# Reordering the units of a decoder layer: when transposed probabilities are copied, where TensorE's side work stands, and when the per-token head maxima are taken

## The reference

```python
x = x + attn(layernorm(x), Wq, Wk, Wv, Wo)        # 16 heads of 32, causal over 512 tokens
x = x + xattn(layernorm(x), ctx, ctx)             # per token: 16 x 16 scores between heads, causal over heads
x = x + ffn(layernorm(x), W_int4, bias, A, B)     # 256 x 256, weights rounded to int4, rank 16 addition

# attn:  scores = q k^T / sqrt(16), causal, softmax, times v, times Wo
# xattn: q[s, q, :] . ctx[s, k, :] / sqrt(16), for each token s on its own, softmax over k, times ctx
```

## Time and profile before

| | us |
|---|---|
| median of 3 runs | 926.34 (923.63 to 928.44) |
| profiled execution, its time | 928.57 |
| its span in the trace | 926.5 |
| granted PE clock, mean over the span | 0.932 |
| busy: PE / weight loads / DVE / ACT / POOL | 711.5 / 576.6 / 631.8 / 611.4 / 480.2 |

### The profile page before, as it was taken

The page is one execution under the profiler, slowest core; times in us unless marked ns, Lnnn a source line. Parts: engine busy times, 40 slices in busy tenths (PEclk is TensorE's granted clock), DMA queues, the critical chain, the costliest instruction groups (busy, mean ns, idle before and its releaser), DMA issues.

```text
span 926.5 us, 15953 instructions
## 1 busy us (share of the span) xinstructions
PE 711.5 (77%) x5147; PEld 576.6 (62%) x5147; DVE 631.8 (68%) x1897; ACT 611.4 (66%) x1688; POOL 480.2 (52%) x449
## 2 busy tenths in 40 slices
PE   3777888777677767787677767787677797779997
PEld 2655667566555555666556555666556575559995
DVE  2544555577477758886568758886568787878873
ACT  4567776987388847877478847877478867762110
POOL 1000001263677664675577664675577847836542
PEclk9789899999799988999989989999989998979997
DMA  5856566576346725576536725576536653500001
GB/s 154 117 70 78 68 101 98 73 100 99 46 65 88 108 42 74 77 118 92 73 48 103 107 42 74 80 116 92 73 49 103 85 88 50 96 7 13 29 12 35
DMA packets 46980, 70.53 MB, mean 76 GB/s; under 512 B 4385, under 2 KB 21554, under 8 KB 46898
## 3 DMA queue, kind: packets, MB, share of 16 engines
q1 hardware_dynamic: 46898, 69.52, 50.3%
HBM read 14.98 MB, written 4.19 MB: 21 GB/s over the span
## 4 chain that ended last, share of the span: by engine, by line
PE 47%; ACT 18%; DVE 14%; issue 10%; POOL 6%; DMA 4%; SPq 1%; ACTq 0%; DVEq 0%; POOLq 0%
PE misc L453 21%; PE score_bank L453 10%; PE acc_bank L453 9%; ACT probs L819 8%; PE turn_bank L539 6%; POOL prod L1459 4%; DVE score_bank L1099 4%; DVE head_scores L1126 4%; DMA stack_k<-k_lo 4%; ACT probs_t L775 3%; PE turn_bank L453 2%; ACT inv_wide L775 1%; DVE attn_t L1121 1%; ACT x_in L782 1%; DVE ln_raw L1079 1%
## 5 line engine op out<-in xcount | busy, mean ns | idle before, releaser
L1099 DVE CUSTOM_DVE_ANT_0 score_bank<-score_bank,causal 128x384 f32<-128x384 f32 (+3 forms) x512 | 242.9, 509 | 113.7 <-PE score_bank L453 113.3
L819 ACT ACTIVATE probs<-score_bank,neg_max 128x384 f32<-128x384 f32 (+3 forms) x512 | 269.1, 538 | 76.8 <-DVE neg_max L1099 76.4
L775 ACT ACTIVATE probs_t<-turn_bank 128x512 f32<-128x512 f32 x320 | 193.9, 606 | 138.8 <-PE turn_bank L539 138.0
L539 PE MATMUL turn_bank<-ident,probs 128*128 128x128 f32 x1280 | 203.7, 283 | 16.0 <-ACT probs_t L775 14.9
L1459 POOL TENSOR_TENSOR prod<-head_probs,ctx_sb 128x256 f32<-128x256 f32 (+1 forms) x100 | 181.5, 1846 | 2.0
L539 PEld LDWEIGHTS turn_bank<-ident,probs 128*128 128x128 f32 x1280 | 150.9, 146 | 43.0 <-issue 29.9
L453 PE MATMUL score_bank<-stack_k,stack_q 96*128 96x384 f32 (+3 forms) x512 | 157.7, 369 | 25.9 <-DMA stack_k<-k_lo 12.7
L263 POOL TENSOR_TENSOR prod<-x1n,ctx_sb 128x256 f32<-128x256 f32 (+1 forms) x104 | 157.5, 1547 | 6.1 <-ACT x1n L782 6.1
L1408 POOL TENSOR_TENSOR ln_var<-ln_mv,eps 128x4 f32<-128x4 f32 x21 | 4.8, 228 | 259.9 <-DVE ln_mv L1087 259.9
L453 PE MATMUL acc_bank<-probs_t,values 128*32 128x384 f32 (+2 forms) x1280 | 79.2, 395 | 40.9 <-ACT probs_t L775 40.9
L819 ACT ACTIVATION_READ_ACCUMULATOR probs<-score_bank,neg_max 128x1 f32 x512 | 110.3, 215 | 0.0
(11 more groups left out here) (171 smaller groups left out, 1262.1 us busy)
## 6 DMA issues: line engine op xcount, KB each, us to landing
stack_q<-q_hi SPq DMA_DIRECT2D x64, 256.0 KB, 5.0
stack_k<-k_hi SPq DMA_DIRECT2D x64, 256.0 KB, 9.7
stack_q<-q_lo SPq DMA_DIRECT2D x32, 256.0 KB, 7.1
stack_k<-k_lo SPq DMA_DIRECT2D x32, 256.0 KB, 11.0
x_in<-in_x SPq DMA_DIRECT2D x9, 512.0 KB, 11.8
ctx_sb<-in_ctx SPq DMA_DIRECT2D x32, 128.0 KB, 2.1
x<-in_x SPq DMA_DIRECT2D x7, 512.0 KB, 7.5
out<-y_sb SPq DMA_DIRECT2D x5, 512.0 KB, 3.2
```

The lines of the kernel that those rows point to most:

```text
L539: last = nc.tensor.transpose(turn_bank[unit % 2][:, j * P:(j + 1) * P], probs[:, unit % RING, j * P:(j + 1) * P], ident[:, :])
L775: return nc.scalar.activation(dst, src, ACT.Identity)
L819: last = nc.scalar.activation(probs[:, unit % RING, at:at + width], score_bank[unit % 3][:, at:at + width], ACT.Exp, bias=neg_max[:, ring, ...
L1099: last = vec.tensor_tensor_reduce(v, v, causal[:, T - width:T], 1.0, 3.0e38, ALU.add, ALU.min, neg_max[:, ring, h, blk:blk + 1])
```

## The change

`LAG` stays 3 for PE's transposes, and a new `KEEP_LAG` of 4 says when ACT copies them: ACT now makes the exponential of unit n first and then copies the transposed unit n - 4. PE's side work is spread so that about one piece stands in a unit: it takes the transposes of a unit ahead of `attend`, moves `attend` to unit 4, `spread_inverses` to unit 6, `project_v` to units 5 and 7, and both halves of the output projection to group 0 units 8 and 9 (before: group 0 unit 9 and group 1 unit 2). The two `misc` banks are dealt out anew. The head maxima are taken in unit 1 of the following group, and POOL subtracts them there after the largest of its four products. The load of `x1` is issued by ACT rather than SP. Some layer norm pieces move by one or two units.

```diff
-    LAG = 3
+    LAG, KEEP_LAG = 3, 4
@@ PE, body
+                        if st["N"] and n < LAG or st["C"] and n >= LAG:
+                            turn_unit()
+                        if st["N"] and n == KEEP_LAG:
+                            attend(st["N"][1])
                         if st["A"] and n in (0, 1):
                             ...
                             project_qk(st["A"][1], n)
-                        if st["N"] and n == LAG:
-                            attend(st["N"][1])
-                        if st["N"] and n < LAG or st["C"] and n >= LAG:
-                            turn_unit()
-                        if st["N"] and n == LAG + 1:
+                        ...
+                        if st["N"] and n == 6:
                             spread_inverses()
-                        if g == 1 and ok(i - 1) and n == 2:
-                            output_projection(1)
...
-                        if g == 0 and ok(i - 1) and n == 9:
-                            pe.wait_ge(attn_ready, n_attn.up(NG))
-                            output_projection(0)
+                        if g == 0 and ok(i - 1) and n in (8, 9):
+                            if n == 8:
+                                pe.wait_ge(attn_ready, n_attn.up(NG))
+                            output_projection(n - 8)
@@ ACT, body
-                        if st["N"] and n < LAG or st["C"] and n >= LAG:
-                            keep_turned((n - LAG) % UNITS)
...
                         if st["C"]:
                             exponential(n, st["C"][1])
+                        if st["N"] and n < KEEP_LAG or st["C"] and n >= KEEP_LAG:
+                            keep_turned((n - KEEP_LAG) % UNITS)
...
+                            nc.scalar.dma_start(x1[:, :, :], x_t[i - 1]).then_inc(x1_loaded, 16)
@@ DVE, body
+                        if attended and n == 1:
+                            head_maxima()
...
-                        if g == 0 and i >= 0 and ok(i + 1) and n in (5, 7):
+                        if g == 0 and i >= 0 and ok(i + 1) and n in (4, 6):
...
+                        if g == 0 and ok(i - 1) and n == 9:
+
+                            dve.wait_ge(x1_loaded, n_x1.up(16))
+                            add_to_x1(0)
...
-                        if scored_tile and n == 9:
-
-                            dve.wait_ge(h_masked, n_masked.now())
-                            vec.tensor_reduce(head_max[:, :], head_probs[:, :, :], axis=AX_X,
-                                              op=ALU.max).then_inc(h_max, 1)
@@ POOL, body
-                        score_products(gp, t, range(CHUNKS)).then_inc(hqk_prod, 1)
+                        score_products(gp, t, (3,))
+                    if attended:
+                        shift_scores()
+                    if scored_tile:
+                        score_products(gp, t, (0, 1, 2)).then_inc(hqk_prod, 1)
```

More of the change, by code:

```diff
@@ L492, in ffn_low_rank, with transpose_tokens @@
                 last.then_inc(setup_pe, 1)
-            def transpose_tokens(src, sem_out, c, reader, count):
-                bank = take(c, reader, count)
+            def transpose_tokens(src, sem_out, c, which, reader, count):
+                bank = take(which, reader, count)
                 for t in range(NT):
@@ L500, in project_qk @@
             def project_qk(g, which):
-                bank = take(which, qk_lo_ready, r_lo)
+                bank = take(1 - which, qk_lo_ready, r_lo)
                 n = 0
@@ L510, in project_v @@
             def project_v(pair, half):
-                bank = take(1 - half, v_ready, r_v)
+                bank = take(1, v_ready, r_v)
                 for t in range(2):
@@ L558, in spread_inverses @@
                 pe.wait_ge(inv_spread, n_group.total)
-                bank = take(1, attn_ready, r_attn)
+                bank = take(0, attn_ready, r_attn)
                 for t in range(NT):
@@ L573, in ffn @@
             def ffn(half):
-                bank = take(half, y_ready, r_y)
+                bank = take(1 - half, y_ready, r_y)
                 for t in range(2):
@@ L617, in body @@
-                        if pair is not None and n in (6, 8):
-                            if i < 0 and n == 6:
-                                pe.wait_ge(w_lo_ready, 2)
-                            project_v(pair, n // 2 - 3)
-                        if (i, g) == (0, 1) and n == 7:
+                        if g == 2 and ok(i + 1) and n in (2, 4):
+                            if n == 2:
+                                pe.wait_ge(ln_done[0], n_ln[0].up(LN_PARTS))
+                            transpose_tokens(x_in, xt_psum, n // 2 - 1, 1, xt_ready, r_xt)
@@ L622, in body @@
+                        if pair is not None and n in (5, 7):
+                            if i < 0 and n == 5:
+                                pe.wait_ge(w_lo_ready, 2)
+                            project_v(pair, n // 2 - 2)
+                        if st["N"] and n == 6:
+                            spread_inverses()
+                        if (i, g) == (0, 1) and n == 8:
                             ffn_largest()
-                        if (i, g) == (0, 1) and n == 8:
+                        if (i, g) == (0, 1) and n == 9:
@@ L800, in keep_values @@
                 copy(values[:, 2 * pair:2 * pair + 2, 2 * half:2 * half + 2, :],
[L801 removed]
+                     misc[1][:, :].rearrange("p (t s n) -> p s t n", t=2, s=2)).then_inc(v_ready, 1)
             def other_weights():
@@ new lines, in body @@
+                        if g == 2 and ok(i + 1) and n in (3, 5):
+                            act.wait_ge(xt_psum, n_xt.up())
+                            copy(xt_hi[:, n // 2 - 1, :], misc[1][:, :]).then_inc(xt_hi_ready, 1)
+                        if st["N"] and n == 5:
+                            keep_acc()
+                        if pair is not None and n in (6, 8):
+                            keep_values(pair, n // 2 - 3)
+                        if g == 1 and ok(i - 3) and n in (8, 9):
+                            act.wait_ge(x2t_psum, n_x2t.up())
+                            copy(x2t_hi[:, n - 8, :], misc[9 - n][:, :]).then_inc(x2t_hi_ready, 1)
@@ L968, in _ @@
                 body(i)
-            for n in range(UNITS - LAG, UNITS):
+            for n in range(UNITS - KEEP_LAG, UNITS):
                 keep_turned(n)
@@ L1160, in body @@
                             take_max(n, st["C"][1])
+                        if g == 1 and ok(i - 1) and n == 0:
+                            add_to_x1(1)
                         if st["A"] and n in (1, 2):
```

152 lines of the change are left out of this document (70 added, 82 removed).

## The result

| | before | after |
|---|---|---|
| median, us | 926.31 (923.63 to 928.44, 4 runs) | 1040.2 (1037.75 to 1041.82, 4 runs) |
| span of the profiled execution | 926.5 | 1035.7 |
| granted PE clock, mean | 0.932 | 0.877 |

The changed kernel takes 1.123 times as long, 95% interval 1.119 to 1.127. The forecast was 917 us and the range 901 to 938, so it was wrong in its sign and far outside its range.

The account below looks back on a forecast made before the run. Chains from engine to engine bound the kernel, with DVE's 8 us wait for POOL. Terms of -21.1 on 928.57 gave 907.5; 12 for path changes and clock gave 919.5; less 2.2 to the median, 917 us, range 901 to 938.

Parts of the forecast that it names:

- the stall: DVE's wait in group 0 until POOL has masked the head scores: 8 us, gone five times, batches 2 to 6.
- the late copy: ACT's copy behind the exponential, one unit later: gives back some 3 us of a batch's gain in g2 and g3.
- a loop over two units: Maxima, exponential, copy, transpose, filler, scores, maxima: 3.37 us for two units of two pieces, plus PE's filler.
- four distances: Attend to attend: about 28 to 30 us in g0, 23 to 25 in g1, 23 to 24.5 in g2 and g3.
- The issue of x1's load: ACT asks for x1 in g0 n3; taken as costing nothing, hidden in slack below some 0.7 us.
- floor: Sums along one path at full clock: 98.4 us a steady batch, 907.5 in all; chance 0.25 that it is met.
- the other path: The path changes between odd and even units where fillers make the other heavier: some 0.5 us in a batch.
- second rival: The loop costs more than the stall gave, with attend at half clock in g0 and g1: 941 us, chance 0.23.
- one stretch in a batch: One further stretch of PE at the lower clock level in each of eight batches, 1 us each.
- a case with the clock at its full level: Without the stall PE would keep 2.4 GHz, so 1 us in each of eight batches is not spent: 909 us.
- Batch 0: The first batch, its groups short of attends and full of weight work: put at -1 us.
- fourth rival: ACT's wait for transposes, 138.0 us, was the real bound; ending it speeds every group: about 885 us, chance 0.07.

Follow-up runs that it names:

- the warm run: Changed kernel with five extra 128 wide matmuls of constants into `acc_bank` ahead of the transposes of unit 3 and of unit 4: 1012.75 us, ratio 1.092.
- the fastest kernel: Changed kernel with `KEEP_LAG` 3 and ACT's copy ahead of the exponential, attend in unit 3 behind the transpose: 856.88 us, ratio 0.920.

## Why the prediction was wrong

**What bounds the kernel, and the stall.** The reading of the stall was right: it goes, the row of `head_max` is gone, and taken alone the edit wins 32 us. That the late copy makes a loop over two units was right too: its links came out within 0.1 us of their forecast sizes, and PE waits for `probs_t` some 1 us in most units, as the prediction said it would. And g2 and g3 got longer, as it said. None of the four distances that it named held, though: 32.5 for 28 to 30 in g0, 26.8 for 23 to 25 in g1, 27.2 and 28.2 for 23 to 24.5. The issue of x1's load, for which it took nothing, takes ACT's queue 0.37 to 0.42 us, seven times.

**The step that failed** is the one behind the sums: "These are sums along one path with nothing else in its way, so they are a floor. Two things come on top", and then "1.5 us in each of eight batches". The measured time is not near that path: in batch 5 the distance to the floor is 114.7 - 98.4 = 16.3 us, not 1.5, and in batches 2 to 6 together 574.2 - 489.7 = 84.5, or 16.9 a batch. The late copy was put at some 3 us in g2 and g3 of a batch; the kernel before with it alone takes 100 us more (1027.6 against 927.8). The chain of one group, g3 to g0, can be read from the timeline above: attend to the maxima of unit 6, 6.81 (572.77 to 579.58); to those of unit 8, 4.91; DVE from there to unit 9, 1.66 (586.15); to those of unit 1, 6.39 (to 592.54); to its exponential 0.80; ACT itself to the exponential of unit 3, 5.26 (forecast 5.28); and to attend, 2.43. That is 28.26 where the forecast had 23.3. Of the 5.0 us between them:

- low clock 3.2: attend 3.54 for 2.30, the projection 2.71 for 1.39, a transpose 1.02 for 0.41. The mean granted clock of this stretch is 0.86, where the earlier trace rows has 1.00.
- the other path 1.8, the rest, of which 1.4 between attend and unit 9. The chain runs over the even units from attend on, not the odd ones, and it has a link that no sum had: the copy of unit 0 waits for attend (89.3 us in 31; here 576.52), then the transpose at 577.26 for the copy, then a projection of the values stands ahead of the scores at 579.15. Before, this copy stood ahead in ACT's unit 3 and waited for an attend of the same unit. Now it stands behind an exponential, in the unit after, with attend behind one more transpose, and PE's next transpose waits for the copy in turn.

For the other groups this wasn't taken apart; they are 3.5, 3.9 and 3.9 us over their floors, so the miss is of one size in all four, but its parts need not be. This is a comparison of lengths along one chain and not a test: the warm run takes attend's share of the clock away, and still stands 12.9 us over the floor in its batch.

**The clock was taken as a small correction to the loop, and it is part of it.** PE's waits of 1 to 1.8 us come just ahead of the transposes and of attend, and then attend, a filler of every group, runs long. I allowed one stretch in a batch. The second rival named this very mechanism, with attend at half clock in two groups, and gave 941; its own test, a clock under 0.85 in g0 and g1, did not come true (0.92 and 0.90). The clock was lowest in g3. By the warm run attend's part is 27 us of the 114. So the second rival had the direction and a part of the mechanism, not the size.

The Trainium skill (TensorE: Matmul & The Clock Gate, "What's actually happening") led me to a case with the clock at its full level, because the stall's end would keep PE busy. The rule on idleness agrees with the trace after, whose mean granted clock is 0.877 against 0.932; I had applied it to the one stall that went and not to the 213 waits that came. The Trainium skill's remark on repeating bubbles (Perfetto Trace Analysis, "Optimization Strategy"), that they can mean too few buffers, fits the 213 waits of 1.05 us. With two banks handed back a unit earlier the same edits take 857 to 878 us, so here the time of the release was enough. Whether a third bank would do as much isn't shown; it wasn't tried.

**Batch 0** was put at -1 without a sum and came out at +20.1. With the copy ahead its batch 1 starts at 130.2 us in the trace and not 147.9, so it is the same loss. I had treated it as short of attends and full of weight work, but the loop doesn't need attend.

**The price of the side work** was not seen either: the spread fillers, which the forecast counted only as weights in the loop, are worth 67 us where the loop isn't bound (926.6 to 859.7, with the statistics a unit earlier in it). ACT's wait for transposes falls from 138.0 us to 58.8 in the fastest kernel. That would fit my fourth rival (0.07, 885 us), which the late copy hides here, but it isn't shown that this wait carries the gain: DVE's wait for `q_hi` falls too, from 68.2 us to 14.7. Which of the moved fillers carries it is open as well.

**What stays open.** How much of the 162 us between `KEEP_LAG` 3 and 4 behind the exponential is waiting and how much the clock that follows it: the warm run shows 27 of clock, PE's waits for copies differ by 149 in the transposes and by 111 with those at attend, and the two overlap. And why the kernel with both lags at 4 takes 68 us more than that with both at 3, with nearly the same waits for copies (73.9 and 75.0 in the transposes, 50.3 and 38.3 at attend) and the same count of units in the loop. Its attends are busy for 109.1 us and not 79.5, so some 30 us of it is their clock. The rest isn't explained.

## What to carry to other kernels

Before moving a hand-over later, write out the loop that it closes (who waits for the buffer, what stands ahead of the release on its engine, and how many stages lie between release and next use), and multiply it by every stage of the kernel: here one unit less made 857 us into 905 with the copy ahead of the exponential, and 878 into 1040 with the copy behind it. A sum along one path through such a loop is a lower bound and not a forecast: look for the second path, and for what else waits for the piece that has grown. And don't price TensorE's work at full clock when it waits in every turn of the loop; here attend ran long behind such waits. An edit of several parts should be taken apart even when it loses, for two of the three parts here were worth 70 us.

## What the runs showed of the hardware

The same forty matmuls of attend took 2.37, 3.61 or 4.49 us, and what TensorE had done just before differed. They took 2.37 behind one idle stretch of 1.25, where the transposes of the units before had waited for no copy (`KEEP_LAG` 3, copy behind). They took 3.61 where the transposes of the last two units had waited 1.20 each, and 4.49, nearly twice 2.37 as at the lower of the clock's two levels (1.2 of 2.4 GHz), where these had waited 1.75 and 1.78. But not each such wait was enough: in the changed kernel an attend behind waits of 0.76 and 1.30 still took 2.37:

```profile
542.88 0.63 PE L532 MATMUL turn_bank<-ident,probs 128*128 128x128 f32 x4 [0.76 <-ACT probs_t L767]
...
545.04 0.63 PE L532 MATMUL turn_bank<-ident,probs 128*128 128x128 f32 x4 [1.30 <-ACT probs_t L767]
545.60 2.37 PE L446 MATMUL acc_bank<-probs_t,values 128*32 128x384 f32 x40
```

Extra matmuls in a group, which compute nothing that is used, can be a gain: twenty matmul instructions in each of 31 groups, busy for 81.6 us, made the kernel 27 us faster. The expectation had been 55 to 90.
